# A two-layer relational GNN on one core: the reciprocal counts of layer two are spread a half-lap ahead, copied by ScalarE into the means' place, and multiplied there

## What is computed

```python
def _rgcn_layer(x, src, dst, edge_type, w_rel, root, bias):
    N = x.shape[0]
    seg = dst * NUM_REL + edge_type
    xs = x[src]
    sums = jax.ops.segment_sum(xs, seg, num_segments=N * NUM_REL)
    cnt = jax.ops.segment_sum(jnp.ones(seg.shape, x.dtype), seg, num_segments=N * NUM_REL)
    mean = (sums / jnp.maximum(cnt, 1.0)[:, None]).reshape(N, NUM_REL, -1)
    return jnp.einsum('nrd,rdo->no', mean, w_rel) + x @ root + bias

h = jax.nn.relu(_rgcn_layer(x, src, dst, edge_type, w_rel1, root1, b1))
out = _layernorm(x + _rgcn_layer(h, src, dst, edge_type, w_rel2, root2, b2))
```

## Time and profile before

| | us |
|---|---|
| median of 3 runs | 3963.51 (3960.76 to 3968.31) |
| the profiled execution | 3968.87 |
| its span | 3967.2 |
| busy: POOL | 2988.3 (75%) |
| busy: PE / its weight loads | 2677.0 (67%) / 1801.4 (45%) |
| busy: DVE | 1872.6 (47%) |
| busy: ACT | 375.5 (9%) |

### The profile page before, as it was taken

One profiled execution on the slowest core, in us unless ns is written; L12 is line 12 of the kernel. 1 busy time (PEld: TensorE's weight loads), 2 busy tenths in 40 slices (PEclk: granted clock), 3 DMA queues, 4 the chain that ended last, 5 costly groups with the idle time before them and its releaser, 6 DMA issues.

```text
span 3967.2 us, 31733 instructions
## 1 busy us (share of the span) xinstructions
PE 2677.0 (67%) x10165; PEld 1801.4 (45%) x10166; DVE 1872.6 (47%) x2588; ACT 375.5 (9%) x399; POOL 2988.3 (75%) x3139
## 2 busy tenths in 40 slices
PE   4776777767777676777766666666665666666666
PEld 3444444444444444444454444444444444444444
DVE  6545545455554554545544343443434444343444
ACT  1010100101001010010100101010010100101000
POOL 7777777777777777777777777777777777777775
PEclk7887878788888887878888878787887887878788
DMA  4222232322323223232222222222222222222222
GB/s 132 77 84 86 78 94 78 94 74 78 95 78 94 74 78 94 78 89 66 81 67 60 66 62 63 62 65 62 62 63 65 63 62 62 65 62 63 62 63 58
DMA packets 151575, 293.69 MB, mean 74 GB/s; under 512 B 61620, under 2 KB 82504, under 8 KB 147959
## 3 DMA queue, kind: packets, MB, share of 16 engines
q0 software_dynamic: 100032, 205.07, 18.2%
q1 hardware_dynamic: 46630, 87.29, 6.7%
q10 hardware_dynamic: 4867, 0.79, 0.1%
HBM read 264.68 MB, written 28.25 MB: 74 GB/s over the span
## 4 chain that ended last, share of the span: by engine, by line
POOL 72%; issue 24%; PE 3%; POOLq 0%; DVE 0%; DMA 0%; ACT 0%; DVEq 0%
POOL rows L1400 72%; PE ps_agg L1820 1%; PE ps_agg L1817 1%; PE ps_out L1900 1%; PE ps_bc L1842 0%; POOLq L1436 0%; DMA rows<-in_x_dram,idx_s 0%; PE ps_out L1895 0%; DVE mean L2253 0%; DMA rows<-table,idx_s 0%; POOLq L1343 0%; POOLq L1430 0%; PE ps_bc L1854 0%; POOL mean L1396 0%; PE ps_out L1908 0%
## 5 line engine op out<-in xcount | busy, mean ns | idle before, releaser
L1400 POOL DMA_INDIRECT rows<-table,idx_s x1563 | 1484.2, 950 | 480.4 <-issue 480.4
L1400 POOL DMA_INDIRECT rows<-in_x_dram,idx_s x1507 | 1442.6, 957 | 459.3 <-issue 459.3
L1817 PE MATMUL ps_agg<-S_first,rows 128*128 128x390 f32 x1564 | 900.1, 666 | 1163.1 <-issue 743.5
L1820 PE MATMUL ps_agg<-S,rows 128*128 128x160 f32 (+2 forms) x4692 | 1244.5, 407 | 0.0
L2209 DVE TENSOR_TENSOR ring<-ps_agg,ring 128x429 f32 (+1 forms) x782 | 457.3, 585 | 1402.7 <-PE ps_agg L1820 696.8
L1820 PEld LDWEIGHTS ps_agg<-S,rows 128*128 128x128 f32 x4692 | 954.4, 243 | 351.2 <-issue 237.4
L1817 PEld LDWEIGHTS ps_agg<-S_first,rows 128*128 128x128 f32 x1564 | 339.6, 245 | 1404.1 <-issue 1049.1
L2195 DVE TENSOR_TENSOR S<-ps_iota,comb_b 128x1200 f32<-128x1200 f32 x392 | 547.6, 1397 | 0.0
L2253 DVE TENSOR_TENSOR mean<-ps_bc,ring 128x896 f32<-128x896 f32 (+2 forms) x284 | 300.7, 1061 | 502.8 <-PE ps_bc L1842 498.5
L1900 PE MATMUL ps_out<-mean,wall 128*128 128x448 f32 (+1 forms) x1120 | 499.8, 573 | 0.0
L1900 PEld LDWEIGHTS ps_out<-mean,wall 128*128 128x128 f32 x1120 | 225.1, 209 | 150.4 <-issue 141.0
(11 more groups left out here) (163 smaller groups left out, 811.8 us busy)
## 6 DMA issues: line engine op xcount, KB each, us to landing
attr<-in_edge_attr_dram SPq DMA_DIRECT2D x27, 1176.0 KB, 8.0
rows<-table,idx_s POOLq DMA_INDIRECT x1563, 2.5
rows<-in_x_dram,idx_s POOLq DMA_INDIRECT x1507, 2.5
x_in<-in_x_dram SPq DMA_DIRECT2D x54, 224.0 KB, 2.6
table<-h_s SPq DMA_DIRECT2D x54, 224.0 KB, 2.3
table<-outT SPq DMA_DIRECT2D x27, 224.0 KB, 3.6
xt_s<-table SPq DMA_DIRECT2D x27, 224.0 KB, 3.5
out_dram<-h_s SPq DMA_DIRECT2D x27, 224.0 KB
```

The lines of the kernel that those rows point to most:

```text
L1400: pool.indirect_dma_start(out=rows[:, o, j, :], out_offset=None, in_=(x, table)[l][:, :], in_offset=bass.IndirectOffsetOnAxis(ap=at, axis= ...
L1817: ins = t_.matmul(sums, lhsT=rows[:, o, jj, :], rhs=S_first[:, PLACE[o], h, :, :], start=True, stop=False)
L1820: ins = t_.matmul(sums[:, :, lo:lo + w], lhsT=rows[:, o, jj, :], rhs=S[:, PLACE[o], h, j - 1, :].rearrange("p (r n) -> p r n", n=WN)[:, :, ...
```

## The change

Layer one and the early and late parts of the last half-lap stay as they are. In layer two, five new things:

- PE spreads the reciprocals of half-lap b during half-lap b itself (`spread_ahead`, `SPREADS_AHEAD`), behind octets 2 to 6, not those of b - 1 during b. Each spread waits until ACT has copied the one before (`rc_taken`), the first one for `cnt_in`.
- ACT copies each spread pair from `ps_bc` into `mean` (`take_counts`), five copies of 128 x 896 per half-lap, placed between its other work.
- In the next half-lap DVE multiplies in place: `mean = mean * ring` (`scale_there`), behind the adds of octet 0 (k = 0), 1 (k = 1 and 2), 2 (k = 3) and 3 (k = 4). In the last half-lap the multiplies keep the places of `END_MEANS`.
- `TYPES` of layer two starts the transform at (2, 0) instead of (2, 1) and has relations 6 and 7 at (4, 0) instead of (4, 1).
- In the last half-lap of layer two the five spreads of its predecessor are gone, since they were made ahead.

```diff
+                def take_counts(b, before, k):
+                    made = before + 2
+                    act.wait_ge(bc_ready[k], made if isinstance(b, int) else act.snap(made))
...
+                    a_.copy(mean[:, 2 * k:2 * k + 2, :], ps_bc[:, :, 0:HN]).then_inc(rc_taken, 1)
...
+                        some_counts = l == 1 and not last
+                        if some_counts:
+                            take_counts(b, before, 0)
                         if not (l == 1 and known and b >= HALVES - 2):
                             act.wait_ge(agg_ready[3], with_it)
...
                             give(b2_, par, 0)
+                        if some_counts:
+                            take_counts(b, before, 1)
+                        if not is_(b, 0) and not last:
+                            clear(1 - par, HN, past)
+                        if some_counts:
+                            take_counts(b, before, 2)
+                            if is_(b, 0):
+                                take_counts(b, before, 3)
+                                take_counts(b, before, 4)
...
                                 take_out(l, b - 1, 0, HN, prev, past, PARTS * 16 if is_(b, 1) else None)
+                                if some_counts:
+                                    take_counts(b, before, 3)
                                 made = b if known else act.snap(before - HALVES)
                                 square(HN, made)
                                 if not last:
                                     root_of_variance(HN, made)
+                                    take_counts(b, before, 4)
...
+                def spread_ahead(b, done, k):
+                    taken, landed = 5 * done + k, 16 * done + 16
...
+                    if k == 0:
+                        pe.wait_ge(cnt_in, landed)
+                        hold(b)
+                    if k or not is_(b, 0):
+                        pe.wait_ge(rc_taken, taken)
+                        hold(b)
+                    spread_to(k)
...
+                SPREADS_AHEAD = {(2, 1): 0, (3, 1): 1, (4, 1): 2, (5, 1): 3, (6, 1): 4}
                 SPREADS = {(1, 0): 0, (2, 0): 1, (2, 1): 2, (3, 1): 3, (4, 0): 4}
-                TYPES = {(2, 1): (-1, 0, 1), (3, 0): (2, 3), (3, 1): (4, 5), (4, 1): (6, 7), (5, 0): (8, 9)}
+                TYPES = ({(2, 1): (-1, 0, 1), (3, 0): (2, 3), (3, 1): (4, 5), (4, 1): (6, 7), (5, 0): (8, 9)},
+                         {(2, 0): (-1, 0, 1), (3, 0): (2, 3), (3, 1): (4, 5), (4, 0): (6, 7), (5, 0): (8, 9)})
...
+                def scale_there(b, par, k, taken):
+                    dve.wait_ge(rc_taken, taken)
+                    hold(b)
+                    here = mean[:, 2 * k:2 * k + 2, :]
+                    v_.tensor_tensor(here, here, ring[:, 2 * k:2 * k + 2, par * HN:par * HN + HN], ALU.mult
+                                     ).then_inc(scaled[k], 1)
...
-                MEANS = {1: 0, 2: 1, 4: 4}, {2: 2, 3: 3}
+                MEANS = {1: (0,), 2: (1,), 4: (4,)}, {2: (2,), 3: (3,)}
+                MEANS_THERE = {}, {0: (0,), 1: (1, 2), 2: (3,), 3: (4,)}
```

More of the change, by code:

```diff
@@ L1185, in gnn_kernel @@
         cnt_in = sem("cnt_in")
+        rc_taken = sem("rc_taken")
         bc_ready = [sem(f"bc_ready{k}") for k in range(5)]
@@ L1221, in gnn_kernel @@
                        *added[3], *added[4], *added[5], *added[6], fold_read, fold_done, cnt_ready, cnt_saved, cnt_in,
-                       *bc_ready, *rc_step, *scaled, ring_zeroed, x_in_done, x_end_in, xt_turned, xt_ready, xt_in, root_done,
+                       rc_taken, *bc_ready, *rc_step, *scaled, ring_zeroed, x_in_done, x_end_in, xt_turned, xt_ready, xt_in, root_done,
                        out_ready, outT_taken, back_turned, h_ready, hT_saved, rows_saved, z_ready, z_sum, z_mid, z_sq,
@@ L1642, in clear @@
                             .to_broadcast([P, R + 1, n])).then_inc(ring_zeroed, 1)
+                def take_counts(b, before, k):
+                    made = before + 2
+                    act.wait_ge(bc_ready[k], made if isinstance(b, int) else act.snap(made))
+                    if not isinstance(b, int):
+                        act.sem_inc(held, 1)
+                    a_.copy(mean[:, 2 * k:2 * k + 2, :], ps_bc[:, :, 0:HN]).then_inc(rc_taken, 1)
                 def take_xt(b, before, with_it):
@@ L1722, in _ @@
                             give(b2_, par, 0)
+                        if some_counts:
[7 more added lines that the diff above has]
+                                take_counts(b, before, 4)
                         if not is_(b, 0):
-                            if not last:
-                                clear(1 - par, HN, past)
                             if l == 0:
@@ L1833, in aggregate, with spread, spread_to @@
                         ins.then_inc(agg_ready[o], 1)
-                def spread(l, k, made, counts):
+                def spread(k, made):
                     if k == 0:
-                        pe.wait_ge(*((cnt_ready, made) if l == 0 else (cnt_in, counts)))
+                        pe.wait_ge(cnt_ready, made)
                     else:
                         pe.wait_ge(scaled[k - 1], made)
+                    spread_to(k)
+                def spread_ahead(b, done, k):
+                    taken, landed = 5 * done + k, 16 * done + 16
+                    if not isinstance(b, int):
+                        taken, landed = pe.snap(taken), pe.snap(landed)
+                    if k == 0:
[4 more added lines that the diff above has]
+                        hold(b)
+                    spread_to(k)
+                def spread_to(k):
                     for c in range(2):
@@ L1929, in first_part @@
                         spread_part(l, 0, EARLY, k, early, ps_bc[:, k % 2, :],
-                                    (scaled[k - 2], early) if k > 1 else (scaled[4], past))
+                                    (scaled[k - 2], early) if k > 1 else
+                                    (scaled[4], past) if l == 0 else (rc_taken, 5 * END))
                         if k == 3:
@@ L1979, in _ @@
                                 spreads = END_SPREADS if last else SPREADS
-                                if some and (o, h) in spreads:
-                                    spread(l, spreads[o, h], past, times)
-                                types = END_TYPES if last else TYPES
+                                if l == 0 and some and (o, h) in spreads:
+                                    spread(spreads[o, h], past)
+                                types = END_TYPES if last else TYPES[l]
                                 if some and (o, h) in types:
@@ L1991, in _ @@
                                     transform(l, 0, HN, types[o, h], past)
+                                if l and not last and (o, h) in SPREADS_AHEAD:
+                                    spread_ahead(b, done, SPREADS_AHEAD[o, h])
                                 if some and (o, h) == ((3, 1) if last else (5, 1)):
@@ L2310, in mend_rows @@
                     v_.tensor_tensor(have, ps_bc[:, :, :], have, ALU.add).then_inc(rows_mended, 1)
-                MEANS = {1: 0, 2: 1, 4: 4}, {2: 2, 3: 3}
-                END_MEANS = {1: 0, 2: 2, 3: 4}, {1: 1, 2: 3}
+                MEANS = {1: (0,), 2: (1,), 4: (4,)}, {2: (2,), 3: (3,)}
+                MEANS_THERE = {}, {0: (0,), 1: (1, 2), 2: (3,), 3: (4,)}
+                END_MEANS = {1: (0,), 2: (2,), 3: (4,)}, {1: (1,), 2: (3,)}
                 dve.wait_ge(ring_clear, 3)
@@ L2337, in _, with taken @@
                         end = l * PARTS + END + 1
+                        def taken(k):
+                            return 5 * (b - 1) + k + 1 if known else dve.snap(nth * 5 + (k - 4))
                         for o in range(OCTS):
@@ L2361, in _ @@
                                     make_S(1 - par, k, (agg_ready[4 + k], with_it))
-                            ahead_of, behind = END_MEANS if last else MEANS
-                            if some and o in ahead_of:
-                                scale(b, 1 - par, 0, HN, ahead_of[o], None if l == 0 and is_(b, 1) else prev, past)
+                            ahead_of, behind = END_MEANS if last else (MEANS, MEANS_THERE)[l]
+                            for k in ahead_of.get(o, ()) if some else ():
+                                if l:
+                                    scale_there(b, 1 - par, k, taken(k))
+                                else:
+                                    scale(b, 1 - par, 0, HN, k, None if is_(b, 1) else prev, past)
                             if o == 5 and not (l == 0 and is_(b, 0)) and not (l == 1 and last):
@@ L2379, in _ @@
                                             None if is_(b, 1) else (prev * 16 if known else dve.snap(prev * 16)))
-                            if some and o in behind:
-                                scale(b, 1 - par, 0, HN, behind[o], None, past)
+                            if some and o == 0 and l:
```

(6 more changed lines are left out.)

## The result

| | us | runs |
|---|---|---|
| before | 3965.91 median (3960.76 to 3968.73) | 4 |
| changed | 4004.4 median (4003.77 to 4009.55) | 4 |
| ratio | 1.0101, 95% interval 1.0084 to 1.0119 | |
| the profiled execution of the changed kernel | 4003.77, span 4002.1 | |

The change makes the kernel 1.0% slower, 38.5 us between the medians and 34.9 between the spans of the two profiled executions.

A forecast was written before the change was run, and what follows sets the result against it. GpSimd's back-to-back gathers bound the kernel. Multiplies +44, L2290's new place -2 and the tail -1 gave +41 us, so 4004 us from a median of 3963.51, range 3984 to 4036.

The forecast's parts named there:

- The bound: GpSimd's gathers run one behind the other, 1563 in layer two; POOL never waits for another engine's semaphore.
- Items 1 and 2: Layer two's 135 multiplies get two SBUF operands, stay at 1.09 us and delay gathers by +41 us, leaned to +44.
- even phases: Multiplies start evenly over the 1.25 us between gathers: mean delay 0.34 us each, 1.51 per half-lap with the pair.
- no slot locked: A multiply's phase follows its octet's last gather, so one of five slots might hit every time (25 us) or never.
- the ratio 1.3: Old two-SBUF operations: 8.7 us of stretch measured against 6.6 by formula; at that ratio the multiplies would cost 53 us.
- Item 3: L2290, now right behind the pair k1, k2, often falls early into a gather: its 2.8 us fall by some 2.
- Items 4 and 5: 135 ScalarE copies of about 1 us are free; moved TensorE spreads, new waits and earlier loads never reach POOL.
- Item 6: The tail: ten spread matmuls (4.5 us) gone from the last half-lap, 0 to -1 us, taken as -1.
- The lock for whole instructions, both ways: Rival: multiply and gather each hold the other out for whole instructions, 106 us, 4067; with bad luck beyond 4036, chance 0.08.
- That a pair keeps the gather out to its end: Milder rival: k1 and k2 both hold the gather, or phases lock unluckily: 60 to 70 us, 4021 to 4031.
- No collision: Rival: copies and in-place multiplies run free beside the gathers, time stays at 3963, chance 0.05.

The follow-up runs named there:

- e5: Changed kernel with its layer-two multiply reading a constant 1 from PSUM in place of the counts in mean: 3965.4 us against 3964.11 before, ratio 1.0005.
- e7: Changed kernel with each 896-column multiply split into two of 448 columns, same results: 3988.67 us, ratio 1.0058 to before.
- e6: Kernel before with its whole half-lap multiply in layer two reading mean (SBUF) in place of ps_bc, no copies added: 4008.95 us, ratio 1.0112.

## Why the prediction was right

- **The bound.** POOL alone, no wait for another engine, an unchanged step: right (waits of POOL above).
- **Items 1 and 2, the multiply.** 1.088 us as forecast (1.09). 41 us by even phases, 40.0 measured; the 1.51 per half-lap was 1.48. The four slots differ (added up from the trace: k = 0 0.28, the pair 0.63, k = 3 0.26, k = 4 0.31 us, where 0.34, 0.49, 0.34 and 0.34 were forecast), and no slot locked. The pair was priced too low and the single ones too high, which cancelled. The lean of 3 us towards the ratio 1.3 was wrong: the worse phases of the old operations said nothing on the new.
- **Item 3.** The place was right, the size was not. L2290 was taken to cost 2.8 us by even phases (26 x 0.108); in the trace of before it stretches the gathers by 5.4 us. Behind the pair, as L2342, it costs 0.3, so 5.1 us went where some 2 were forecast. L2271, now L2323, went from 2.9 to 1.5 us, which was not forecast. The fold (now L2264) stands right behind the pair in every second half-lap and the prediction left it out: it cost nothing in layer two before, and 2.4 us now. The operations with two SBUF operands after the pair had to be counted all, not one of them.
- **Items 4 and 5.** The copies take 0.90 us and are free (e5). ScalarE's late copies and the earlier loads reach nobody on the chain (e5). VectorE's 339 us of waiting for ps_bc are gone and stand now in front of its adds (1078 us idle there for 708): it follows the gathers either way.
- **Item 6.** The tail lost 1.1 us, forecast 1.
- **The sum, and luck.** 4004 hit 4004.4 closer than its parts deserve. The gathers of layer two were to grow by 44 - 2 = 42 us and grew by 36.9: the multiplies 4 less than forecast, item 3 and L2271 some 4.5 less, the fold 2.4 more, small shifts some 1 more. Between the profiled executions the growth is 34.9 us, not 41 (4003.77 for the 4009.9 forecast). Between the medians it is 38.5, and the median of before, 3963.51 in the prediction, is 3965.91 with its fourth run, which hides the 2.5 that are missing. The kernel's own runs differ by 6 us. The mechanism carries the forecast; the last few us are luck.
- **The rivals.** The lock for whole instructions, both ways (4067), is out: the multiply at 2944.22 began inside a gather and neither was held, and of the 135 multiplies all 89 that began inside one took 1.08 to 1.11 us. That a pair keeps the gather out to its end is out by e7, where the gather gets in after the first half. No collision (3963) is out by e6. By the Trainium skill (SBUF — State Buffer, "Who interferes with whom") a VectorE instruction with two SBUF inputs contends with a GpSimd instruction that reads SBUF; e5 and e6 are that sentence on this kernel, both ways. The prediction repeats the section's other half, no contention with at most one SBUF input, without the condition that the Trainium skill sets there, outside the 2-port perf modes; the cast above reads one SBUF tensor and does stretch a gather. The Trainium skill infers in the same section that a tensor_tensor leaves descriptor generation alone; for these indirect gathers, whose indices are in SBUF, e6 shows 45 us of stretch beside one. Whether the reading of the indices is held or another part of the gather was not separated.

## What to carry to other kernels

Where gathers on GpSimd are the bound, count the SBUF operands of every VectorE instruction beside them: in these runs one operand in PSUM was free, and two in SBUF cost about (D - 0.17)^2 / (2 x 1.25) us each for an instruction of D us, with 1.25 us from gather to gather. So long ones hurt most and cutting them helps. The formula is an estimate for even phases: it held for the sum of many, and a single slot of the half-lap was off by up to 0.23 us. Look at casts from SBUF to SBUF as well. Here, moving an operand from PSUM to SBUF to take a wait off an engine that nobody waits for bought nothing and paid this. And look whether the bound is the same on another chip before a gain of a per cent is believed.

## What the runs showed that was not expected

The same program took 3964 us on one chip and 4629 to 4632 on three others, with the same length of one gather (0.94 us) and the same step (0.30), and there with some 143 waits of POOL for PE, 3.8 us on the mean. On those chips neither 22 us more nor 22 us less of GpSimd's work moved the time by more than 0.2%.

Also, two VectorE instructions that follow at once overlap by 0.08 us (2.11 us for two of 1.09 in the timeline of the changed kernel), and a gather still gets in after the first. Still, a pair back to back is no bargain: it cost 0.63 us per half-lap, more than two of the single multiplies (0.26 to 0.31 each).
